# A two-layer transformer decoder on one core: the context's turns, products and Gram matrix moved from the projection stage into two units of self-attention

## What is computed

```
def _L0_xattn_ref(context, mem0, W0, W1, mask):
    m = (mask == 0)[:, None, :]
    u = mem0
    for W in (W0, W1):
        key_ = jnp.einsum('bpd,md->bpm', u, W)
        attn = jnp.einsum('bpm,blm->bpl', key_, context)
        attn = jnp.where(m, neg_inf, attn)
        w = jax.nn.softmax(attn, axis=-1)
        o = jnp.einsum('bpl,bld->bpd', w, context)
        u = u + o
    return u
...
x = _layernorm(x + _L0_attn_ref(x, ...), axis=-1)
x = _layernorm(x + _L0_xattn_ref(ctx_1024, x, L0_xattn_W0, L0_xattn_W1, mask_BxS2_if1), axis=-1)
x = _layernorm(x + _L0_ffn_ref(x, ...), axis=-1)
x = _layernorm(x + _L1_attn_ref(x, ...), axis=-1)
x = _layernorm(x + _L1_xattn_ref(x, ctx_1024, ctx_1024, ...), axis=-1)
x = _layernorm(x + _L1_ffn_ref(x, ...), axis=-1)
```

## Time and profile before

| what | value |
|---|---|
| time, median of 3 runs | 782.1 us (781.95 to 782.55) |
| span of the profiled execution | 777.6 us |
| instructions | 10965 |
| PE busy | 710.5 us (91%) |
| PE weight loads busy | 386.9 us (50%) |
| DVE busy | 494.3 us (64%) |
| ACT busy | 559.6 us (72%) |
| POOL busy | 193.9 us (25%) |

### The profile page before, as it was taken

One profiled execution on the slowest core, in us unless ns is written; L12 is line 12 of the kernel. 1 busy time (PEld: TensorE's weight loads), 2 busy tenths in 40 slices (PEclk: granted clock), 3 DMA queues, 4 the chain that ended last, 5 costly groups with the idle time before them and its releaser, 6 DMA issues.

```text
span 777.6 us, 10965 instructions
## 1 busy us (share of the span) xinstructions
PE 710.5 (91%) x3850; PEld 386.9 (50%) x3850; DVE 494.3 (64%) x1169; ACT 559.6 (72%) x1101; POOL 193.9 (25%) x246
## 2 busy tenths in 40 slices
PE   4999999989999999999999999889999899992797
PEld 2642222212222224889788886544555644441686
DVE  4794645653412223578547666858877687988786
ACT  3659999999999995464142345799987533798991
POOL 1751242201010000203353242555544100000022
PEclk9999999999999999999999999999999999997799
DMA  7422112141256160303336000010100000000002
GB/s 196 136 39 43 28 28 72 24 96 28 42 134 191 29 183 0 110 0 110 108 109 217 1 0 1 1 60 22 42 1 0 1 1 0 1 0 0 1 27 82
DMA packets 57390, 42.14 MB, mean 54 GB/s; under 512 B 36882, under 2 KB 54136, under 8 KB 57208
## 3 DMA queue, kind: packets, MB, share of 16 engines
q1 hardware_dynamic: 57192, 41.31, 19.0%
q10 hardware_dynamic: 144, 0.13, 0.1%
HBM read 28.59 MB, written 4.46 MB: 42 GB/s over the span
## 4 chain that ended last, share of the span: by engine, by line
PE 54%; ACT 25%; DVE 15%; issue 3%; DMA 1%; SPq 1%; POOL 0%; POOLq 0%; ACTq 0%; DVEq 0%
ACT arena L655 12%; PE banks L1668 9%; PE banks L2217 8%; PE banks L1972 7%; PE banks L1988 6%; ACT arena L780 4%; PE banks L1654 4%; PE banks L1638 3%; DVE arena L1493 2%; PE banks L1828 2%; PE banks L2105 2%; DVE arena L1055 2%; DVE arena L1063 2%; PE banks L2002 1%; PE banks L1711 1%
## 5 line engine op out<-in xcount | busy, mean ns | idle before, releaser
L655 ACT ACTIVATE arena<-banks 128x1024 f32<-128x1024 f32 x256 | 239.7, 1047 | 6.5 <-PE banks L1668 4.0
L1668 PE MATMUL banks<-arena 128*32 128x512 f32 x1024 | 136.4, 604 | 2.6 <-DVE arena L1131 2.4
L1654 PE MATMUL banks<-arena 64*128 64x512 f16 x512 | 86.4, 383 | 10.1 <-ACT arena L655 5.8
L2217 PE MATMUL banks<-arena 128*128 128x512 f32 x192 | 83.1, 594 | 1.1 <-DVE arena L1509 0.9
L780 ACT ACTIVATE arena<-banks,arena 128x77 f32<-128x77 f32 x256 | 70.2, 392 | 10.5 <-DVE arena L1408 10.4
L398 POOL TENSOR_SCALAR arena<-arena 128x2 f32<-128x2 f32 (+2 forms) x39 | 11.8, 302 | 255.5 <-DVE arena L1058 255.5
L1654 PEld LDWEIGHTS banks<-arena 64*128 64x128 f16 x512 | 20.9, 93 | 108.6 <-ACT arena L655 99.0
L736 ACT ACTIVATE arena<-banks,arena 128x256 f32<-128x256 f32 x64 | 26.9, 471 | 49.3 <-PE banks L1972 49.3
L2217 PEld LDWEIGHTS banks<-arena 128*128 128x128 f32 x192 | 36.2, 190 | 47.4 <-issue 43.4
L1988 PE MATMUL banks<-arena 128*128 128x256 f32 x256 | 56.5, 380 | 1.2 <-ACT arena L677 1.2
L1972 PE MATMUL banks<-arena 128*128 128x256 f32 x256 | 56.2, 379 | 0.0
(11 more groups left out here) (265 smaller groups left out, 1275.2 us busy)
## 6 DMA issues: line engine op xcount, KB each, us to landing
arena<-in_L_ffn_w SPq DMA_DIRECT2D x16, 1024.0 KB, 7.5
w_kept<-arena SPq DMA_DIRECT2D x3, 768.0 KB, 3.7
arena<-w_kept SPq DMA_DIRECT2D x3, 768.0 KB, 4.7
arena<-in_x SPq DMA_DIRECT2D x4, 512.0 KB, 6.9
out_x<-arena SPq DMA_DIRECT2D x3, 512.0 KB, 2.9
arena<-in_L_ffn_b SPq DMA_DIRECT2D x1, 1024.0 KB, 8.7
arena<-in_L_ffn_w_gate SPq DMA_DIRECT2D x1, 768.0 KB, 7.7
arena<-in_L_ffn_w_up SPq DMA_DIRECT2D x1, 768.0 KB, 9.4
```

The source lines that it names most:

```text
L655: act.activation(PT[kt % 2][:, half], PS[:, 2 * (n % 3):2 * (n % 3) + 2, :], ACT.Exp, scale=DH ** -0.5 / QK_UP ** 2).then_inc(sem("exp_don ...
L1654: mm = pe.matmul(bank(2 * (n % 3) + h), KT[u % 2][64 * h:64 * h + 64, P * kt:P * kt + P], QT[u % 2][64 * h:64 * h + 64, 512 * half:512 * h ...
L1668: mm = pe.matmul(PS[32 * j:32 * j + 32, 6, :], VS[w][:, kt, h, :], PT[kt % 2][:, half, h, :], start=(kt == 0), stop=(kt == TB - 1))
L2217: mm = pe.matmul(bank(2 + n % 4), (wgT if n < IC * G4 else wuT)[:, k, P * c:P * c + P], XT[:, k, 512 * g:512 * g + 512], start=(k == 0), s ...
```

## The change

The three pieces leave the head. `context_turned`, `context_hops` and `context_gram` become helpers of DVE, called in units 6 and 7 behind `quantised` and the late tiles' work and ahead of the copy of bank 6. PE gets `context_step`, called behind `values` in each step of these two units (`step` counts from 0 to 15 over both): the turns at step 0, hop 0's products at steps 4 and 5, hop 1's at steps 9 and 10, the Gram products at step 13. All write bank 7 alone, so each piece waits until DVE has read the one before it. The turned context and the turned vectors now share one signal, and the output projection waits for the Gram copy.

```diff
@@ vector engine
+            def context_turned():
+                mask()
+                dve.wait_ge(sem("vec_tr"), 1)
+                dve.tensor_copy(ctxT, bank(7)[:, 0:KD * B * LC].rearrange("p (k l) -> p k l", k=KD)).then_inc(sem("mem_ctxT"), 1)
+                dve.tensor_copy(vecT, bank(7)[:, KD * B * LC:KD * B * LC + E * FT + 6 * KD]).then_inc(sem("vec_T"), 1)
+            def context_hops(k):
+                dve.wait_ge(sem("mem_mask"), 1)
+                dve.wait_ge(sem("mem_cw_mm"), k + 1)
+                dve.tensor_tensor(CWT[:, k], bank(7)[:, 0:2 * B * LC].rearrange("p (i l) -> p i l", i=2),
+                                  keepm[:, None, :].to_broadcast([P, 2, B * LC]), ALU.mult).then_inc(sem("mem_cw"), 1)
+            def context_gram():
+                dve.wait_ge(sem("mem_g_mm"), 1)
+                dve.tensor_copy(Gm[0:LC], bank(7)[0:LC, 0:B * LC].rearrange("p (b l) -> p b l", b=B)).then_inc(sem("mem_g"), 1)
@@ attn_unit(u)
                 if late < T and u % 2 == 1:
                     late_v(late)
+                if u == NP - 2:
+                    context_turned()
+                    context_hops(0)
+                if u == NP - 1:
+                    context_hops(1)
+                    context_gram()
                 if u >= NP:
@@ the head
                 biased(t)
-                if t == 4:
-                    mask()
...
-                if t == 6:
-
-                    dve.wait_ge(sem("mem_mask"), 1)
-                    for k in range(KD):
...
-                if t == 8:
...
@@ matrix engine
+            def context_turn():
+                pe.wait_ge(sem("mem_in"), 16 * 5)
+                pe.wait_ge(sem("v_evac"), T)
...
+            def context_hop(k, hop):
+                if hop == 0:
+                    pe.wait_ge(sem("mem_cw") if k else sem("vec_T"), 1)
+                    pe.wait_ge(sem("mem_ctxT"), 1)
+                for m in range(KD):
+                    mm = pe.matmul(bank(7)[:, B * LC * hop:B * LC * hop + B * LC], Wmem[:, hop, m, P * k:P * k + P], ctxT[:, m, :],
+                                   start=(m == 0), stop=(m == KD - 1))
+                if hop == 1:
+                    mm.then_inc(sem("mem_cw_mm"), 1)
...
+            def context_step(step):
+                if step == 0:
+                    context_turn()
+                if step in (4, 5):
+                    context_hop(0, step - 4)
+                if step in (9, 10):
+                    context_hop(1, step - 9)
+                if step == 13:
+                    context_gram()
@@ attn_unit(u)
                     values(u, kt)
...
+                    if NP - 2 <= u < NP:
+                        context_step(step)
```

More of the change, by code:

```diff
@@ L1136, in _ @@
                 biased(t)
-                if t == 4:
-                    mask()
[L1140 to L1143, removed]
-                if t == 6:
-                    dve.wait_ge(sem("mem_mask"), 1)
-                    for k in range(KD):
-                        dve.wait_ge(sem("mem_cw_mm"), k + 1)
-                        dve.tensor_tensor(CWT[:, k], bank(6 + k)[:, 0:2 * B * LC].rearrange("p (i l) -> p i l", i=2),
-                                          keepm[:, None, :].to_broadcast([P, 2, B * LC]), ALU.mult).then_inc(sem("mem_cw"), 1)
-                if t == 8:
-                    dve.wait_ge(sem("mem_g_mm"), 1)
-                    dve.tensor_copy(Gm[0:LC], bank(6)[0:LC, 0:B * LC].rearrange("p (b l) -> p b l", b=B)).then_inc(sem("mem_g"), 1)
                 if 2 <= t <= TB:
@@ L1695, in first_turn @@
                 else:
-                    pe.wait_ge(sem("v_evac"), T)
+                    pe.wait_ge(sem("mem_g"), 1)
                     pe.wait_ge(sem("o_evac"), NP)
@@ L1721, in first_out, with context_gram @@
                     first_proj(q, (step - 11) // 2, (step - 11) % 2)
+            def context_turn():
+                pe.wait_ge(sem("mem_in"), 16 * 5)
+                pe.wait_ge(sem("v_evac"), T)
+                for k in range(KD):
+                    for b in range(B):
+                        pe.transpose(bank(7)[:, B * LC * k + LC * b:B * LC * k + LC * b + LC], ctxv[0:LC, b, P * k:P * k + P], ident[0:LC, 0:LC])
+                pe.wait_ge(sem("vec_in"), 16 * 7)
+                nv = E * FT + 6 * KD
+                pe.transpose(bank(7)[:, KD * B * LC:KD * B * LC + nv], vraw[0:nv, :], ident[0:nv, 0:nv]).then_inc(sem("vec_tr"), 1)
+            def context_hop(k, hop):
[7 more added lines that the diff above has]
+                    mm.then_inc(sem("mem_cw_mm"), 1)
+            def context_gram():
+                pe.wait_ge(sem("mem_cw"), KD)
+                for b in range(B):
+                    for k in range(KD):
+                        mm = pe.matmul(bank(7)[0:LC, LC * b:LC * b + LC], ctxT[:, k, LC * b:LC * b + LC], CWT[:, k, 1, LC * b:LC * b + LC],
+                                       start=(k == 0), stop=(k == KD - 1))
+                mm.then_inc(sem("mem_g_mm"), 1)
+            def context_step(step):
[7 more added lines that the diff above has]
+                    context_gram()
             def attn_unit(u):
@@ L1744, in _ @@
                 project(t)
[L1745 to L1772, removed]
             pe.wait_ge(sem("qk_biased"), HT)
```

## The result

The changed kernel took 789.24 us in the median of 4 runs (787.67 to 791.45), the kernel before 782.33 beside it (781.95 to 783.51). The ratio is 1.0096, with a 95% interval of 1.0071 to 1.0121: the change costs about 7 us. The forecast was slower, 787.3, with a range of 784.7 to 789.2. The sign and the main mechanism came out as told. Against the forecast of 787.3 that is 1.9 and 1.4 us more.

What follows compares the result with a forecast made beforehand. Self-attention was taken as bound by ACT with PE close behind, the head by PE alone. 782.1 - 2.8 (head) + 5.9 (stall) + 1.9 (clock) + 0.2 (unit 7) = 787.3 us, range 784.7 to 789.2.

Steps and rivals of the forecast that it cites:

- The pause: Unit 6, step 4: PE stands from 157.6 to 163.9, 6.3 us, until DVE's copies behind `late_qn` are done.
- Exponential 112: Unit 7's first exponential starts at 168.1 instead of 162.16, 5.9 us late, before the low clock's cost.
- The clock: Unit 6: granted clock falls in the pause, returns 4.3 us after PE resumes, costing 1.9 us, between 0 and 2.8.
- The price of a product: Units 6 and 7: two hop products cost PE 0.53 us, a quarter of the head's 2.10.
- Unit 7: Hop 1's and the Gram products fit the unit's 2.1 us of room; 0.2 us lost, between 0 and 0.6.
- The head: Removing the three pieces starts self-attention 2.8 us earlier, between 2.2 and 3.0; first exponential near 52.2.
- The range: Whole kernel: 784.7 (head gain 3.0, stall 0.3 shorter, unit 7 0) to 789.2 (the costlier rival).
- The 4.5 us around the span: Timed median 782.1 less profiled span 777.6, taken as time around the span that the change leaves alone.
- DVE is in time: Unit 6: copies signal before 157.6, PE doesn't wait, kernel is faster at 779.5 us; chance 0.05.
- the stall is halved: Unit 6: 3 us of stall left, clock doesn't fall, 782.1 us, no change; chance 0.05.
- the clock costs little: Unit 6: stall as forecast, but clock stays up or returns at once, 785.4 us; chance 0.22.
- it costs more: Low clock lasts longer (2.8), head gains only 2.2, unit 7 loses 0.6: 789.2 us; chance 0.08.

Runs made afterwards that it cites:

- early copies: Changed kernel with DVE's mask and copies of the turned context ahead of the quantisation and `late_qn` of tile 15 in unit 6: 779.93 us, ratio 0.9983.
- late products: Changed kernel with PE's products moved behind DVE's copies (steps 8, 9, 11, 12, 14) and hop 0's masked product in unit 7: 781.79 us, ratio 0.9997.
- pause alone: Kernel before, context work in its head, plus a PE wait in unit 6 for four small DVE copies behind `late_qn`: 790.31 us, ratio 1.0100.

## Why the prediction was right in kind, and what was mis-sized

**The pause** was predicted at 6.3 us, on the first product of hop 0, released by DVE's second copy, behind a list of DVE without idle time. It measured 6.15 in both profiles of the changed kernel. The early copies and the late products show that this distance makes the loss. The kernel with the pause alone shows that the pause is enough for it: 6.81 us of it, with the low clock, lengthened unit 6 by 7.25.

**Exponential 112** was to be 5.9 us late for the pause and 1.9 for the clock, 7.8 in all. Unit 6 grew by 8.42 and 7.92 us. Without the clock it is 6.4 instead of 5.9; the price of a product, below, is most of the missing half.

**The clock** fell, came back 4.4 and 3.3 us after the resumption (4.3 in the earlier trace rows), and cost 1.5 to 2.0 against a term of 1.9. The row of an idle stretch elsewhere in the same trace was a good price for this one. The factor of two that the Trainium skill's page "TensorE: Matmul & The Clock Gate" gives between the clocks ("Back-to-back issue gap") is nearly what the group of values shows: 1.93 us at a granted clock of 0.50 and 1.06 at 1.00, a factor of 1.8.

**The price of a product.** I took 0.53 us for two products of 154 columns, a quarter of the group of eight in the head. On their own between values and scores they hold PE for 0.73 (158.90 to 159.63 in the early copies). Within a run of its kind the product was cheaper here than between others. The two pairs in unit 6 make 0.4 of the missing 0.5.

**Unit 7** is the first step that failed: "all 1.6 us fit into the unit's 2.1 us. I take 0.2 for the two neighbouring steps, between 0 and 0.6". The unit took 1.00 us more in every profile with the products at steps 9 and 10: exponential 122 came 0.80 later by the two steps, exponential 128 1.00 later; from exponential 134 on 0.73 of it was left. By rows, such a step is 1.00 + 0.54 + 0.73 = 2.27 us against 1.81 of ACT, 0.46 over; twice that is 0.9. The room of the steps before didn't count; my reading, which no run separates, is that PE can't run ahead by more than the scores in hand. Two steps apart, the unit itself cost 0.55, but by exponential 134 it was 0.95.

**The head** is the second: "I bound the gain between 2.2 ... and 3.0, and take 2.8". It was 1.4 to 2.0, so this is the larger part of the miss, and the first exponential, told for 52.2, came at 57.66 and 54.38. I had named the danger, that normalising over DVE, ACT and POOL might keep tiles from following, and allowed 0.3 us for it. DVE's waits for POOL's L411 grew from 0.4 to 3.2 us, POOL's three lines now hold 41% of the head's chain, and added POOL work costs this head about twice what it cost the old one. With the products gone from PE, the ring over POOL sets part of the pace.

**The range** had a bound for each of the failed terms, and both terms were outside theirs on the same side, the head by 0.2 to 0.8 us, unit 7 by 0.4 (0.1 if counted to exponential 134). From the measured pieces: -1.7 for the head, +8.2 for unit 6, +1.0 for unit 7, -0.3 for the exponentials behind it, together +7.2, against +6.9 and +6.4 in the two comparisons.

**The 4.5 us around the span** were misread, without harm to the sum. Every later execution took 1.7 to 1.9 us more than its span. So the one with the span of 777.6 took about 779.4, by that estimate, 2.7 us less than the median: the profile showed a quick execution, with early bias rows and no low clock in its head.

**The rivals.** That DVE is in time, that the stall is halved, and that the clock costs little all fell. The other end, "it costs more", came closest with its 789.2, by other terms than the ones that it named: a smaller gain in the head and the cost in unit 7, not a longer spell of low clock.

## What to carry to other kernels

When work is moved to where an engine has room, look at the engine that feeds it as well: PE had 2 us of room in each of units 6 and 7, but its product waits for a copy that DVE's list reaches 6 us later, and all that stands behind the product waits too. Write down, for each wait that is moved, when each side reaches it; moving either side past the other cured it here.

Price a small operation where it will stand, between others of another kind, and count room step by step rather than over a unit. And don't book the whole of what is taken off the path in one stage without asking which ring of engines runs only a little faster; one profile of a head whose start hangs on a DMA is one draw among several.

## What I had not expected of the hardware

The same head, instruction for instruction, had its first exponential at 54.97 and at 59.34 us. PE's wait ahead of tile 2 was 0.57 us in the one and 3.58 in the other, and with the longer one the clock was low for 6.8 us, and tile 2's product for q and k took 3.78 us instead of 1.98. Bias rows that landed 1.7 us later thus went with a self-attention that began 4.4 us later.

The landing alone doesn't decide it. Two profiles of the changed head both had it at 14.84; in one PE waited 1.58 us, the clock stayed up and the first exponential came at 54.38, in the other PE waited 2.66 us, the clock was low for 3.4 us and it came at 55.88. Over the eleven profiles, the clock stayed up with waits of 0.57 and 1.58 us, was low for 3.4 us with waits of 1.95 to 2.66, and for 6.8 us with 3.02 and 3.58. These are the rows of this head, not a rule.
